# Decoder kernel on one core: output bias as a matmul, softmax shift inside the exponential, norm transposes ahead of the stage boundary

## The reference, cut to what matters

```
x = _layernorm(x + _L0_attn_ref(...))     # stage A: 32 heads of 16, ALiBi bias, causal, output bias
x = _layernorm(x + _L0_xattn_ref(...))    # stage B: 32 query heads of 128 on 8 key/value heads, rotary
x = _layernorm(x + _L0_ffn_ref(...))      # stage C: base weight plus top-2 of 8 low-rank experts
x = _layernorm(x + _L1_attn_ref(...))     # stage D: 32 query heads of 128, sliding window
x = _layernorm(x + _L1_xattn_ref(...))    # stage E: single-head cross attention with 512 features
x = _layernorm(x + _L1_ffn_ref(...))      # stage F: quantised gate/up/down with low-rank parts
```

```
scores = einsum('bhqd,bhkd->bhqk', q, k) * SCALE
scores = where(causal, scores + bias, -inf)
attn = softmax(scores, axis=-1)
out = einsum('bhqk,bkhd->bqhd', attn, v).reshape(B, S, HIDDEN)
return out @ w_proj + b_proj
```

## Time and profile before

| | us |
|---|---|
| median of 3 runs | 1686.52 |
| lowest and highest | 1686.01, 1686.56 |
| the profiled execution | 1692.06 |
| its span | 1690.1 |
| TensorE busy | 1588.4 (94%) |
| VectorE busy | 987.8 (58%) |
| ScalarE busy | 660.3 (39%) |
| GpSimd busy | 202.4 (12%) |

### The profile page before, as it was taken

The page is one execution under the profiler, slowest core; times in us unless marked ns, Lnnn a source line. Parts: engine busy times, 40 slices in busy tenths (PEclk is TensorE's granted clock), DMA queues, the critical chain, the costliest instruction groups (busy, mean ns, idle before and its releaser), DMA issues. The chain is left out here.

```text
span 1690.1 us, 22766 instructions
## 1 busy us (share of the span) xinstructions
PE 1588.4 (94%) x8504; PEld 1276.1 (76%) x8504; DVE 987.8 (58%) x1948; ACT 660.3 (39%) x1193; POOL 202.4 (12%) x146
## 2 busy tenths in 40 slices
PE   8688699999999999999889999999999999989998
PEld 6565487787788778876777788788878877767876
DVE  5996777766765776677433442552553346246755
ACT  4475434433343443333333332332332323426541
POOL 8321040000000000000340000000000000703330
PEclk9899999999999999999999999999999999999999
DMA  6010011101110110100111110110110100202231
GB/s 231 29 45 30 5 59 51 61 15 39 38 50 1 63 50 13 38 13 26 45 52 38 38 51 1 61 50 12 50 54 21 38 13 25 77 10 73 77 92 50
DMA packets 26023, 75.44 MB, mean 45 GB/s; under 512 B 3888, under 2 KB 4624, under 8 KB 25680
## 3 DMA queue, kind: packets, MB, share of 16 engines
q1 hardware_dynamic: 25552, 73.16, 13.0%
q0 software_dynamic: 384, 1.05, 0.2%
HBM read 72.10 MB, written 2.10 MB: 44 GB/s over the span
## 5 line engine op out<-in xcount | busy, mean ns | idle before, releaser
L83 PE MATMUL bankY<-sb_Bwo,sb_BoT 128*128 128x512 f32 x768 | 194.4, 403 | 0.3 <-DVE sb_BoT L1077 0.3
L83 PE MATMUL bankY<-sb_Dwo,sb_DoT 128*128 128x512 f32 x768 | 192.3, 399 | 0.3 <-DVE sb_DoT L1077 0.3
L83 PE MATMUL bankA<-sb_xT,sb_Bwq 128*128 128x512 f32 x768 | 190.7, 397 | 1.1 <-issue 1.1
L83 PE MATMUL bankA<-sb_xT,sb_Dwq 128*128 128x512 f32 x768 | 189.9, 396 | 0.0
L83 PEld LDWEIGHTS bankY<-sb_Bwo,sb_BoT 128*128 128x128 f32 x768 | 141.6, 190 | 42.5 <-issue 13.2
L83 PEld LDWEIGHTS bankY<-sb_Dwo,sb_DoT 128*128 128x128 f32 x768 | 139.8, 188 | 41.7 <-issue 13.3
L83 PEld LDWEIGHTS bankA<-sb_xT,sb_Bwq 128*128 128x128 f32 x768 | 142.3, 188 | 35.7 <-issue 4.4
L83 PEld LDWEIGHTS bankA<-sb_xT,sb_Dwq 128*128 128x128 f32 x768 | 142.2, 188 | 33.9 <-issue 2.7
L1008 DVE TENSOR_TENSOR sb_BqT<-bankA,sb_Btable 128x512 f32<-128x512 f32 x64 | 44.2, 691 | 151.2 <-ACT sb_Bsw L905 151.2
L1044 DVE TENSOR_TENSOR sb_xtok<-sb_xtok,bankY 128x512 f32<-128x512 f32 x128 | 87.1, 681 | 53.7 <-PE bankY L83 53.6
L905 ACT ACTIVATE sb_Bsw<-bankA 64x512 f32<-64x512 f32 x160 | 94.7, 592 | 54.9 <-PE bankA L83 51.7
(11 more groups left out here) (273 smaller groups left out, 2985.8 us busy)
## 6 DMA issues: line engine op xcount, KB each, us to landing
sb_raw<-in_w_attn SPq DMA_DIRECT2D x80, 512.0 KB, 3.5
sb_raw<-in_q_gu SPq DMA_DIRECT2D x22, 256.0 KB, 2.7
sb_raw<-in_q_d SPq DMA_DIRECT2D x11, 256.0 KB, 2.6
sb_raw<-in_wqk SPq DMA_DIRECT2D x8, 256.0 KB, 2.6
sb_rawx<-in_xT SPq DMA_DIRECT2D x4, 512.0 KB, 5.9
sb_raw<-in_ctxT SPq DMA_DIRECT2D x4, 512.0 KB, 6.2
sb_xtok<-in_x_tok SPq DMA_DIRECT2D x1, 2048.0 KB, 12.9
sb_raw<-in_ctx_tok SPq DMA_DIRECT2D x4, 512.0 KB, 3.7
```

What stands on the lines that cost most here:

```text
L83: last = nc.tensor.matmul(out, lhs, rhs, start=start and i == 0, stop=stop and i == len(pairs) - 1)
```

## The change

Three edits.

1. The bias is no longer added to `xtok`. It is loaded once into partitions 0 and 32 of a small tile, rounded to fp32r by ScalarE in both, and the remainder is put into partition 32 by VectorE. A matmul of a tile of ones (96 by 128) with this tile (96 by 512, zero elsewhere) opens the output product of every tile.
2. The scores are negated (`alibi` comes negated from the host), VectorE takes the minimum of them, which is the negated maximum, and the exponential has scale -1. For units 3, 5, ..., 23 and 24 to 31 (`shifted`) VectorE does not subtract; ScalarE makes eight exponentials of 128x64, one per head, with the minimum as the per-partition operand `bias`.
3. `ln_tensor` makes the transposes of tiles 0 to 3 at the end of the stage before (`EARLY`), into `bankT` and `bankA`; tiles 4 to 7 follow in the new stage, into `bankY` and `bankT`. The first products wait until the low parts of the tiles in the banks that they use are made.

```diff
-    ln_banks = [bankT[0], bankT[1], bankY[0], bankY[1]]
+    ln_banks = [bankT[0], bankT[1], bankA[0], bankA[1], bankY[0], bankY[1], bankT[0], bankT[1]]
+    EARLY = range(4)
...
-    def ln_tensor(pe, n):
-        for t in range(NT):
+    def ln_tensor(pe, n, tiles=range(4, NT)):
+        for t in tiles:
             wait_normalised(pe, n, t)
-            if t >= 4:
-                pe.wait_ge(ln_low, n * NT + t - 3)
+            if t >= 6:
+                pe.wait_ge(ln_low, n * NT + t - 5)
...
+        shifted = lambda n: n >= LAST_CHUNK or (n >= 2 and n % 2 == 1)
...
-                sp.dma_start(bp[:], io["bp"].to_broadcast([P, D])).then_inc(small, 16)
+                for r in (0, 32):
+                    sp.dma_start(bpr[r:r + 1], io["bp"]).then_inc(small, 16)
...
+                        nc.gpsimd.memset(f32(ones[:]), 1.0).then_inc(pones, 1)
+                        pool.wait_ge(pones, 1)
+                        nc.gpsimd.memset(f32(bp[:]), 0.0).then_inc(pones, 1)
+                        pool.wait_ge(pones, 2)
...
+                    if t == 0:
+                        pe.wait_ge(pbias, 3)
+                    product(bankY[t % 2][:], [(ones[:], bp[:])], stop=False)
...
                 output_last(NT - 1)
+                ln_tensor(pe, 0, EARLY)
...
                 def exp(n):
-                    act.wait_ge(st["sub"], n + 1)
-                    tile = sc[n % 3][:].rearrange("p j k -> p (j k)")
-                    nc.scalar.activation(tile, tile, ACT.Exp).then_inc(st["exp"], 1)
+                    if shifted(n):
+                        act.wait_ge(st["max"], n + 1)
+                        for j in range(HEADS):
+                            done = nc.scalar.activation(sc[n % 3][:, j, :], sc[n % 3][:, j, :], ACT.Exp, bias=mx[:, n % 2, j:j + 1], scale=-1.0)
+                        done.then_inc(st["exp"], 1)
+                    else:
+                        act.wait_ge(st["sub"], sum(not shifted(i) for i in range(n + 1)))
+                        tile = sc[n % 3][:].rearrange("p j k -> p (j k)")
+                        nc.scalar.activation(tile, tile, ACT.Exp, scale=-1.0).then_inc(st["exp"], 1)
...
+                act.wait_ge(pones, 2)
+                for r in (0, 32):
+                    nc.scalar.activation(bp[r:r + 1, :], bpr[r:r + 1, :], ACT.Copy).then_inc(pbias, 1)
                 exp(0)
...
-                    nc.vector.tensor_reduce(mx[:, n % 2, :], s3, AXX, ALU.max).then_inc(st["max"], 1)
-                    yield
-                    dve.wait_ge(st["max"], n + 1)
-                    nc.vector.tensor_tensor(s3, s3, mx[:, n % 2, :].unsqueeze(2).to_broadcast([P, HEADS, S]), ALU.subtract).then_inc(st["sub"], 1)
+                    nc.vector.tensor_reduce(mx[:, n % 2, :], s3, AXX, ALU.min).then_inc(st["max"], 1)
+                    if not shifted(n):
+                        yield
+                        dve.wait_ge(st["max"], n + 1)
+                        nc.vector.tensor_tensor(s3, s3, mx[:, n % 2, :].unsqueeze(2).to_broadcast([P, HEADS, S]), ALU.subtract).then_inc(st["sub"], 1)
...
+                dve.wait_ge(pbias, 2)
+                nc.vector.tensor_tensor(bp[32:33, :], bpr[32:33, :], f32(bp[32:33, :]), ALU.subtract).then_inc(pbias, 1)
                 dve.wait_ge(in_tok, 16)
-                for t in range(NT):
-                    nc.vector.tensor_tensor(xtok[:, t, :], xtok[:, t, :], bp[:], ALU.add).then_inc(pbias, 1)
...
-                            tiles = {"V": 2 * n + 2, "K": NT // 2 * (n % 2 + 1), "Q": NT // 2 * (n // 4 + 1), "S": NT // 2}[kind]
+                            tiles = {"V": max(2 * n + 2, 4), "K": NT // 2 * (n % 2 + 1), "Q": NT // 2 * (n // 4 + 1), "S": NT // 2}[kind]
```

More of the change, by code:

```diff
@@ L147, in ln_follow, with ln_low_parts, ln_high_parts @@
             nc.vector.tensor_scalar(xtok[:, t, :], xtok[:, t, :], rstd[:, t:t + 1], offset[:, t:t + 1], ALU.mult, ALU.add).then_inc(ln_last, 1)
[L149 to L150 removed]
+    def ln_low_parts(dve, n, tiles=range(NT)):
+        for t in tiles:
             dve.wait_ge(ln_high, n * NT + t + 1)
[L152 removed]
+            nc.vector.tensor_tensor(xT[1][:, :, t * P:(t + 1) * P], ln_banks[t][:].rearrange("p (k c) -> p k c", k=KC),
                                     f32(xT[0][:, :, t * P:(t + 1) * P]), ALU.subtract).then_inc(ln_low, 1)
[L155 to L156 removed]
+    def ln_high_parts(act, n, tiles=range(NT)):
+        for t in tiles:
             act.wait_ge(ln_tr, n * NT + t + 1)
             nc.scalar.activation(xT[0][:, :, t * P:(t + 1) * P],
[L159 to L162 removed]
+                                 ln_banks[t][:].rearrange("p (k c) -> p k c", k=KC), ACT.Copy).then_inc(ln_high, 1)
+    def ln_tensor(pe, n, tiles=range(4, NT)):
+        for t in tiles:
             wait_normalised(pe, n, t)
[L164 to L165 removed]
+            if t >= 6:
+                pe.wait_ge(ln_low, n * NT + t - 5)
             for k in range(KC):
[L167 removed]
+                done = nc.tensor.transpose(ln_banks[t][:, k * P:(k + 1) * P], xtok[:, t, k * P:(k + 1) * P], ident[:])
             done.then_inc(ln_tr, 1)
@@ L408, in output_early @@
                     pe.wait_ge(e_low, 2 * (t + 1))
-                    product(bankY[t % 2][:], [x for k in range(KC - 1) for x in three([w[:, k, :] for w in oS[t % 2]], [w[:, k, :] for w in wbig])], stop=False)
+                    if t == 0:
+                        pe.wait_ge(pbias, 3)
+                    product(bankY[t % 2][:], [(ones[:], bp[:])], stop=False)
+                    product(bankY[t % 2][:], [x for k in range(KC - 1) for x in three([w[:, k, :] for w in oS[t % 2]], [w[:, k, :] for w in wbig])], start=False, stop=False)
                 def output_last(t):
@@ L418, in _ @@
                         scores(t - 3)
-                pe.wait_ge(small, 80)
+                pe.wait_ge(small, 96)
                 for n in range(UNITS):
@@ L508, in _ @@
                     queries(0, h)
-                act.wait_ge(small, 80)
+                act.wait_ge(small, 96)
+                act.wait_ge(pones, 2)
+                for r in (0, 32):
+                    nc.scalar.activation(bp[r:r + 1, :], bpr[r:r + 1, :], ACT.Copy).then_inc(pbias, 1)
                 exp(0)
@@ L590, in residual @@
                     ln_follow(dve, 0, t)
-                dve.wait_ge(small, 80)
+                dve.wait_ge(small, 96)
                 nc.vector.tensor_scalar(row[:], pos[:], 0, ROPE_ROWS - 1, ALU.max, ALU.min).then_inc(clamped, 1)
@@ L843, in start @@
                         for x in START:
+                            if rope and x == ("V", 0):
+                                pe.wait_ge(ln_low, norm * NT + 4)
                             if rope and x[0] == "V":
@@ L1284, in pieces @@
                             pe.wait_ge(w_low, 2 * (1 - a) + m // 2 + 1)
+                        if n < 2:
+                            pe.wait_ge(ln_low, 3 * NT + 3 + n)
                         if a == 0:
@@ L1623, in layouts @@
     heads = 8 * np.arange(KC)[None, :, None, None] + local[:, None]
-    a["alibi"] = bias[heads].transpose(0, 4, 1, 2, 3, 5).reshape(P, KC, D)
+    a["alibi"] = -bias[heads].transpose(0, 4, 1, 2, 3, 5).reshape(P, KC, D)
     a["own"] = np.tile(np.repeat(np.eye(4, dtype=np.float32), A_HD, 0), (2, 1))
```

13 lines of the change are left out of this document (7 added, 6 removed).

## The result

The changed kernel takes 1692.8 us (median of 6, 1688.4 to 1694.8), the kernel before 1686.3 on the same chip: ratio 1.0038, 95% interval 1.0027 to 1.0050, so +6.5 us instead of -9. Taken once more on another chip: 1693.1 against 1687.4, 1.0030 (1.0018 to 1.0041). The profiled execution took 1694.8 us (span 1692.9).

The account below looks back on a forecast made before the run. TensorE, busy 94% of 1690.1 us, was taken as the bound, so only its waits could be won. First attention -2.1 and boundaries -7.3 gave -9.4, applied to the 1686.52 median: 1677 us; 8-in-10 range 1669.5 to 1686.

Parts of the forecast that it names:

- the ring of the unit loop: First attention: a four-unit cycle of 14.59 us closed by ScalarE's program order; TensorE waits for it twice per period.
- step 1: First attention: without the bias additions VectorE starts unit 2 earlier; 12 us gained, 0.5 us paid for matmuls.
- the later of my two cases: Subtraction of unit 4 at 56.8 us rather than 54.3, putting the copy of unit 3 at 61.5, 10.6 us gained.
- on the path: +0.5 us: Bias matmuls, 0.25 us per output tile: six lie in TensorE's waits, those of tiles 6 and 7 cost +0.5 us.
- step 2: First attention: maximum of 19 units moves into eight-piece exponentials, +1.40 us each; loop +8.35, last chunk +2.8, pause -1.75.
- the pieces do not overlap: Rival in ScalarE's ring of the unit loop: 0.337 us per piece, 1689 us in all; chance of slower 0.12.
- together +1.85 per period: Unit loop: exp(6), queries and scores 1.40 us later, plus 0.45 us before exp(8), in each four-unit period.
- the pause: ScalarE's 4.66 us standstill before 161.49 us, last chunk of first attention; may vanish or stay, half taken: -1.75 us.
- the fourth period: Unit-loop period with the last context split's stall, which hides half of the shift's cost: +0.95 us instead of +1.85.
- The last chunk: End of first attention, VectorE and ScalarE form the ring: 6.94 instead of 6.24 us a unit, four units, +2.8 us.
- step 3: Five stage boundaries: early transposes bring first products 8.4 us earlier, lower TensorE clock returns 1.1; -7.3 us.
- No change: Rival: head start only 10.6 us, pause stays, boundaries gain only 3 us; -2 us in all, 1684.5 us; chance 0.13.

Follow-up runs that it names:

- kernel 4: Changed kernel with all edits of the shifted exponential taken back (bias product and early transposes stay): 1674.8 us, ratio 0.9927 to the kernel before.
- experiment 1: Kernel before with the bias edits alone: 1682.7 us, ratio 0.9971.
- experiment 2: Kernel before with the early transposes alone: 1681.3 us, ratio 0.9959.
- kernel 6: Kernel before with the four transposes of unit 0 done three times (8 more TensorE instructions): 1691.8 us, ratio 1.0021.
- Experiment 3: Kernel before with the shifted exponential alone: 1704.2 us, ratio 1.0094.
- kernel 7: Changed kernel with the shift in units 3, 5 to 23 only: 1685.1 us, ratio 0.9984 to the kernel before.
- kernel 8: Changed kernel with the shift in units 24 to 31 only: 1682.4 us, ratio 0.9972 to the kernel before.
- Experiment 10: Kernel 4 with early transposes repeated at all five boundaries, two or three times each, to close TensorE's gap: 1675.4 us, ratio 0.9913 to the kernel before.
- 14: Changed kernel with twelve early transposes of the first boundary done twice: 1686.8 us, ratio 0.9998 to the kernel before.
- Kernel 5: Kernel 4 with the sixteen early transposes of the first boundary done twice: 1671.6 us, ratio 0.9904 to the kernel before.
- 9: Changed kernel with the sixteen early transposes of the first boundary done twice: 1687.5 us, ratio 0.9978 to the kernel before.
- 12: Kernel 4 with eight early transposes of the first boundary done twice: 1683.5 us, ratio 0.9956 to the kernel before.
- 13: Changed kernel unaltered, run again on the same chip as 14: 1693.1 us, ratio 1.0030 to the kernel before.

## Why the prediction was wrong

Forecast -9.4, measured +6.5. By the runs of the parts: bias +6.7 off, shift +7.2, boundaries +1.1; the parts together differ by another 0.9 from the whole. Two steps failed in the mechanism: the path of the longer exponential through the ring of the unit loop, and the cost of the eight matmuls, which lies in the next stage's instruction fetch.

**The bias additions (step 1; -11.5 forecast, -4.8 measured).** The chain went as worked out: the multiplication of unit 1 came at 47.5 in kernel 4 (47.3 forecast), that of unit 2 at 52.8 (52.0) and took 2.38 us beside a split, the subtraction of unit 4 at 57.0, the later of my two cases. So the copy of unit 3 came at 62.4 to 62.8 (experiments 1, 4 and the changed kernel; 61.3 to 62.5 in the other profiles), not at the mean of 59.0 and 61.5 that I took: 9.0 to 9.7, not 12. The one-row subtraction on VectorE took 2.26 us where I had 0.7, beside a split as well. The step that failed outright is the cost of the eight matmuls, "on the path: +0.5 us": they cost 0.2 us at most where they stand (12.03 us from the copy of unit 31 to the next stage in experiment 1, 11.81 in 2), and 2 to 3 us in the next stage (2.7 in experiment 1 against 2 and 3 by the table's last column; 2.1 in 6, the same count of matmuls with no change of the data flow; its whole time grew by 3.5). The two terms make some 4 to 6 of the 6.7 us; the rest isn't placed. Nothing in my sum looked at instruction fetch, though the trace of before had the row: two issue waits of 1.1 us in all behind the loop's jumps, and 19 instruction packets in the loop.

**The shift (step 2; +9.4 forecast, +16.6 measured).** The price of a piece was right (337 ns, eight in 2.01 us), so the rival "the pieces do not overlap" is wrong, although its time, 1689, was nearest; that it was so is luck. What failed is what hung on it, "together +1.85 per period". Experiment 3 against experiment 2, neither with the pause: the five periods take 17.33, 16.56, 17.33, 19.53 and 18.92 us against 14.60, 14.54, 14.61, 18.46 and 14.55, together +12.9 instead of +8.35. The quiet second period is +2.02, near the 1.85. The first and third are +2.7: the subtraction beside the GpSimd split, 0.77 more; I had looked for such a meeting in the fourth period alone (+1.07, forecast +0.95). The fifth is +4.37: 2.97 of it in kernel 7 too, about 1 us of that TensorE's lower clock, which no term of mine held inside the loop; and 1.40 is exp(24), a unit of the last chunk whose exponential runs inside the last loop period; I had counted it in neither (kernel 8, with exp(24) as the only shifted one of that period: 15.92 us, +1.37). The last chunk (copy of unit 23 to 31) is +3.8, forecast +2.8. And the pause, for which I took -1.75, was in the one profile of the kernel before and, it seems, not in its median: on three chips with like times (1687.4 to 1688.3) none of ten profiles has it. So nothing could be won. 4.55 + 1.0 + 1.75 = 7.3, the whole miss.

**The boundaries (step 3; -7.3 forecast, -6.2 measured).** Right in mechanism and, within 1.1 us, in size. The first products came 8.4 us earlier; GpSimd's block limits them at the second, third and fourth boundary as named, the transposes themselves, at the lower rate, at the first and the last in the changed kernel (elsewhere GpSimd's block is up to 0.5 us later at the first). The clock gave back most in one place, the fourth stage: 1.8 to 2.2 us in nine of twelve profiles with early transposes, 1.5 in 10, nothing in 7 and 14; up to 0.8 in the second stage and 0.7 in the last come to it. I had about a quarter of a microsecond in each of four. So the small sum is in part luck. Experiment 10 adds that filling the gap ahead doesn't keep the clock up there while GpSimd's block is late.

**The rivals.** "No change" had two of its three conditions met (a head start near its 10.6, and nothing won at the pause); the third not, as the boundaries gained 6.2 us and not 3. The result was beyond it all the same, because of the loop terms. None of the rivals held the fetch stall. The range ended at 1686, with 0.12 for slower: the bounds were those of the piece's price, and the number of pieces of the ring that could be late beside a GpSimd split wasn't in them.

**The level.** Right to subtract the 5.5 us from the sum; wrong to keep a term (the pause) that could only be in the 5.5.

**The best version.** Kernel 5, the bias and the transposes without the shift and with the loop moved off the stall: 1671.6 us, 1.0% under the kernel before (0.9904, 0.9889 to 0.9919), where the changed kernel is 0.4% over it.

## What to carry to other kernels

Before a waiting engine is given less work, ask which engine closes the ring: here VectorE gave 0.69 us and ScalarE paid 1.40, and everything queued behind the longer instruction moved with it. Look at "issue" waits behind a loop's jump before and after every edit ahead of the loop; if the number of matmuls between jump and stall has shrunk, a dozen harmless instructions more may take the stall away (eight made it longer here), and the instruction packets of the DMA view tell whether a loop is reloaded. And never book as a gain a row that explains why a profiled execution is longer than the median.

## What the hardware showed that was not expected

- The length of a program ahead of a loop sets a stall inside it: about 1, then 3 to 4, then 4.9, then 0 us with 0, 8, 16 and 20 more matmuls ahead. The stall ends 2.2 to 2.9 us after an instruction packet of 16 KB starts at the jump; the kernels without it have no such packet in the loop. The loop of the fourth stage, the same code at another address, never had a stall, though it reloads (16 to 19 packets) in kernels 5, 9 and 14.
- A wait of about 2 us on TensorE can cost as much again in the clock, and not in every execution: the 24 last output products of the second and fourth stage, each behind the same wait of 2.21 us, took 8.10 and 5.73 us before and 7.36 twice after (granted clock 0.68, 1.00, 0.77 and 0.77).
- The two-input operations of VectorE beside a GpSimd split took 1.46, 2.26 (one row of 512) and 2.38 us instead of 0.69. The Trainium skill (SBUF — State Buffer, "SBUF: two separate sides") has the engine that starts first hold the shared ports for its whole instruction; these three agree: each ended 0.54 to 0.55 us after the split that had begun before it.
- Eight exponentials of 128x64 with a per-partition bias, 337 ns each, are 0.24 us apart. By the figures of the Trainium skill (ScalarE: Activation LUTs, "What ACT_TABLE_LOAD costs") it would be 280 + 53 = 333 ns and 0.24: the trace agrees.
- ScalarE's pause beside the indirect gathers (4.7 us) doesn't come with every execution: it is there in four of sixteen profiles, in part in one, absent in eleven. All four profiles of the chip of 9 to 12 have it, whole or in part, none of the ten of the chips of 1 to 8, 13 and 14. The kernel before has it in its profile, kernel 6, which differs by eight matmuls, has not.
